# A fused adapter-linear and state-space kernel: an odd output sum moved ahead of a filter part, the next input loaded earlier, adapter sums held in the rows of their low part

## What is computed

```python
x = x + (einsum('bsd,od->bso', x, W) + bias + einsum('bsr,bor->bso', einsum('bsd,brd->bsr', x, A[ids]), B[ids]))
K = 2 * einsum('hn,hnl->hl', Ct, exp(dtA[:, :, None] * arange(L))).real      # 64 filters of 1024 taps
y = irfft(rfft(x, 2L) * rfft(K, 2L))[..., :L] + x * D[:, None]               # causal convolution
x = x + y * (arange(L) < length)
```

## Time and profile before

| | |
|---|---|
| median of 3 runs | 1104.22 us (1104.08 to 1106.7) |
| the profiled execution's own time | 1102.59 us |
| its span | 1100.9 us |
| mean granted TensorE clock | 0.998 |
| busy: PE, DVE, ACT, POOL | 97%, 77%, 65%, 2% of the span |
| DMA | 284.62 MB, mean 259 GB/s |

### The profile page before, as it was taken

How to read it: one execution, slowest core, us unless ns; L and a number is a source line. 1 busy time by engine, 2 the same in 40 slices (tenths; PEclk the granted TensorE clock), 3 DMA queues, 4 the chain that set the end, 5 groups by cost and what they waited for, 6 DMA issues and landing times.

```text
span 1100.9 us, 21550 instructions
## 1 busy us (share of the span) xinstructions
PE 1067.3 (97%) x8088; PEld 1031.4 (94%) x8088; DVE 848.3 (77%) x1263; ACT 715.7 (65%) x1260; POOL 27.4 (2%) x79
## 2 busy tenths in 40 slices
PE   9999999999999999999999999999999999999998
PEld 7999999999988999999999999999989999999997
DVE  7888877778687786768786777868478888888886
ACT  5655546655737546546647556556498888888885
POOL 0000000000000000000000000000000000000000
PEclk9999999999999999999999999999999999999999
DMA  8557768766867878867877868868799787879773
GB/s 306 192 180 290 259 197 280 230 258 211 288 176 284 245 254 274 231 230 230 269 236 247 253 234 285 232 231 250 264 306 356 285 338 282 344 270 357 280 274 132
DMA packets 162586, 284.62 MB, mean 259 GB/s; under 512 B 10739, under 2 KB 125620, under 8 KB 149044
## 3 DMA queue, kind: packets, MB, share of 16 engines
q1 hardware_dynamic: 162484, 283.26, 75.8%
HBM read 193.96 MB, written 89.26 MB: 257 GB/s over the span
## 4 chain that ended last, share of the span: by engine, by line
PE 68%; DVE 15%; ACT 7%; issue 4%; SPq 4%; DMA 2%; DVEq 0%; ACTq 0%
PE acc L1795 23%; PE acc L1955 23%; PE acc L1801 11%; DVE x_lo L1089 5%; PE acc L1723 4%; PE acc L1990 3%; PE acc L1767 2%; DVE x_sb L1245 2%; ACT L844 1%; DMA x_raw<-x_t 1%; ACT L857 1%; ACT t_hi L686 1%; SPq L436 1%; SPq L444 1%; SPq L440 1%
## 5 line engine op out<-in xcount | busy, mean ns | idle before, releaser
L686 ACT ACTIVATE acc<-acc 128x512 f32<-128x512 f32 x93 | 54.1, 584 | 129.4 <-PE acc L1801 129.1
L1795 PE MATMUL acc<-t_hi,w_pair 128*128 128x256 f32 x960 | 122.9, 280 | 7.0 <-issue 7.0
L1955 PE MATMUL acc<-u_hi,f_hi 128*128 128x512 f32 (+1 forms) x320 | 128.9, 403 | 0.0
L1795 PEld LDWEIGHTS acc<-t_hi,w_pair 128*128 128x128 f32 x960 | 116.8, 188 | 8.2 <-issue 8.2
L1795 PE MATMUL acc<-t_hi,v_lo 128*128 128x256 f32 x512 | 123.0, 279 | 0.0
L1795 PE MATMUL acc<-t_hi,v_hi 128*128 128x256 f32 x512 | 122.9, 279 | 0.0
L1955 PE MATMUL acc<-u_lo,f_hi 128*128 128x512 f32 (+1 forms) x320 | 118.3, 370 | 0.0
L1955 PE MATMUL acc<-u_hi,f_lo 128*128 128x512 f32 (+1 forms) x320 | 118.2, 369 | 0.0
L1089 DVE TENSOR_TENSOR x_lo<-x_raw,x_hi 128x512 fp32r<-128x512 f32 x128 | 79.9, 686 | 49.0 <-ACT x_hi L686 49.0
L1089 DVE TENSOR_TENSOR t_lo<-t_raw,t_hi 128x1024 fp32r<-128x1024 f32 x64 | 78.3, 1224 | 50.1 <-ACT t_hi L686 49.4
L1795 PE MATMUL acc<-x_hi,v_hi 128*128 128x256 f32 x384 | 93.6, 283 | 14.5 <-DVE x_sb L1245 14.3
(11 more groups left out here) (205 smaller groups left out, 2656.8 us busy)
## 6 DMA issues: line engine op xcount, KB each, us to landing
w_pair<-weight_scratch SPq DMA_DIRECT2D x71, 1024.0 KB, 6.2
x_scratch<-x_sb SPq DMA_DIRECT2D x32, 1024.0 KB, 6.3
out<-out_sb SPq DMA_DIRECT2D x63, 512.0 KB, 4.7
x_raw<-x_t SPq DMA_DIRECT2D x15, 2048.0 KB, 9.9
u_raw<-x_scratch SPq DMA_DIRECT2D x14, 2048.0 KB, 11.9
wq_raw<-state_scratch SPq DMA_DIRECT2D x16, 1024.0 KB, 7.8
a_raw<-lora_a SPq DMA_DIRECT2D x128, 64.0 KB, 1.9
b_raw<-lora_b SPq DMA_DIRECT2D x128, 64.0 KB, 2.3
```

The lines of the kernel that those rows point to most:

```text
L686: return act.activation(dst, src, ACT.Copy)
L1795: pe.matmul(by_row(bank_part(bank, i)), w[:, k, i, :], hi[:, k, :, :], start=opens and i == 0 and k == 0 and s == 0, stop=False, skip_grou ...
L1955: mm = pe.matmul(bank, w, m, start=first and i == 0, stop=last and i == 2, skip_group_check=onto_closed)
```

## The change

SP: the next x is loaded right after the S4 load of a group (x of group 1 ahead of the even blocks), the S1 load goes ahead of the A rows, and filter_stores(g, 2) and (g, 3) wait until after the B rows of the next group. ACT: four of the eight x_hi copies go ahead of the T4 split, seed_e(1) behind it; filter_step(g, 2) and (g, 3) behind seed_b(0) of the next group; in group 1 seed_c goes ahead; in the second stage take_state(3, 0) goes ahead of the residual of head 4. DVE: out_12(1) ahead of filter_step(g, 2). `h_own` leaves the x1 buffer and lies in the first rows of `hl`, so `take_h` no longer waits for the odd half's store, and the two subtractions of `split_h` wait for both copies and run one after the other.

```diff
-    h_own = place("h_own", [R2, N], F32, at=x1_at + X1_BYTES)
+    hl_at = cursor[0]
     hl = place("hl", [P, N], F32R)
+    h_own = place("h_own", [R2, N], F32, at=hl_at)
...
             load_filter_inputs()
+            load_x(1)
             load_blocks()
-            load_x(1)
...
                     load_b(i, row)
+                filter_stores(g - 1, 2)
+                filter_stores(g - 1, 3)
                 store_x1(g - 1, 1)
                 load_ws(g, S4)
                 if g < LAST:
+                    load_x(g + 1)
                     rows = [adapter_of(g + 1, i) for i in range(G)]
+                load_ws(g, S1)
+                if g < LAST:
                     sp.wait_ge(c_alo, 2 * (g + 1))
                     for i, row in enumerate(rows):
                         load_a(i, row)
-                load_ws(g, S1)
                 if g == 1:
                     store_sum(S4, 0)
                 filter_stores(g, 0)
-                if g < LAST:
-                    load_x(g + 1)
-                else:
+                if g == LAST:
...
                     store_x1(g, 0)
-                    filter_stores(g, 2)
-                    filter_stores(g, 3)
...
             def take_h(g):
                 act.wait_ge(m_h, 2 * (g + 1))
                 if g > 0:
-                    act.wait_ge(st_x1[1], 16 * g)
+                    act.wait_ge(m_21[1], g)
...
                 if p == 0:
                     act.wait_ge(c_blo, 2 * (g + 1))
                     act.wait_ge(st_x1[0], 16 * g)
-                else:
-                    act.wait_ge(c_hlo, 2 * (g + 1))
+                elif g > 0:
+                    act.wait_ge(st_x1[1], 16 * g)
...
+            for t in range(HALF):
+                split_x(1, t)
             take_p5(1, 0)
-            for t in range(NT):
+            for t in range(HALF, NT):
                 split_x(1, t)
             for g in range(1, n_groups):
                 out_21(1, g - 1)
                 seed_b(0, g)
+                filter_step(g - 1, 2)
+                filter_step(g - 1, 3)
...
                 if g == 1:
+                    seed_c(0, g)
+                    seed_c(1, g)
                     split_even(S3)
                 split_t(g, "T3")
                 if g == 1:
                     split_even(S1)
-                seed_c(0, g)
-                seed_c(1, g)
+                else:
+                    seed_c(0, g)
+                    seed_c(1, g)
...
                 seed_e(0, g)
+                if g < LAST:
+                    for t in range(HALF):
+                        split_x(g + 1, t)
+                split_t(g, "T4")
                 seed_e(1, g)
-                split_t(g, "T4")
                 filter_step(g, 1)
                 if g < LAST:
                     take_p5(0, g)
-                    for t in range(NT):
+                    for t in range(HALF, NT):
                         split_x(g + 1, t)
...
                 take_p5(1, g)
-                filter_step(g, 2)
-                filter_step(g, 3)
...
             split_filter(4)
+            take_state(3, 0)
             residual_early(4)
             residual_late(4)
-            for h in range(3, heads):
+            take_state(3, 1)
+            split_u_early(5)
+            split_u_late(5)
+            split_states(3, 0, 2)
+            split_filter(5)
+            take_state(3, 2)
+            split_states(3, 2, 3)
+            residual_early(5)
+            residual_late(5)
+            for h in range(4, heads):
...
             def split_h(g):
-                dve.wait_ge(c_hhi, 2 * g + 1)
-                for rows in (slice(0, R2), slice(R2, P)):
-                    minus_hi(hl[rows, :], h_own[:, :], hh[0:R2, :]).then_inc(c_hlo, 1)
+                dve.wait_ge(c_hhi, 2 * g + 2)
+                minus_hi(hl[R2:P, :], h_own[:, :], hh[0:R2, :]).then_inc(c_hlo, 1)
+                dve.wait_ge(c_hlo, 2 * g + 1)
+                minus_hi(hl[0:R2, :], h_own[:, :], hh[0:R2, :]).then_inc(c_hlo, 1)
...
             split_t(0, "T4")
+            for t in range(HALF):
+                split_x(1, t)
             out_12(1, 0)
-            for t in range(NT):
+            for t in range(HALF, NT):
                 split_x(1, t)
...
-                if g == 1:
-                    out_12(1, g)
-                    filter_step(g, 2)
-                else:
-                    filter_step(g, 2)
-                    out_12(1, g)
-                    filter_step(g, 3)
+                out_12(1, g)
+                filter_step(g, 2)
+                filter_step(g, 3)
```

## The result

| | before | changed |
|---|---|---|
| median of the runs (20 of each, same chip), us | 1103.55 | 1093.90 |
| lowest to highest, us | 1101.02 to 1106.70 | 1088.75 to 1103.87 |
| the profiled execution, us | 1102.6 | 1096.84 |
| its span, us | 1100.9 | 1095.1 |

The ratio is 0.9919, with a 95% interval of 0.9901 to 0.9938. The change gains about 9 us where the prediction had 25; 1093.9 lies above its range of 1075 to 1088. The changed kernel's 20 runs also scatter over 15 us, the 20 of the kernel before over 6.

The account below looks back on a forecast made before the run. PE is busy 97% of the span, so only its gaps can be won: 16.1 + 2.1 + 1.9 + 3.75 + 1.2 = 25.0 us off a 1104.2 us median gives 1079 us; 8 in 10 for 1075 to 1088.

Parts of the forecast that it names:

- Part 3: x loaded earlier: A22 lands in time for p4(0) in group 10, 2.1 us won; S1 and A rows behind x cost nothing.
- The other waits at p5(0) stay: PE's remaining waits at p5(0), ended by the chain from A-row split to taps, stay: 3.1 us not won.
- group 6: Stalls at end_11 and p5(0), behind a DVE and ACT chain that shortens: 1.9 us won beyond the out_12(1) term.
- Part 1: out_12(1) ahead of the third filter part on DVE: eleven PE waits at p1(1) go whole, 16.1 us.
- Part 4: Four x_hi copies ahead of the T4 split on ACT: they fit in idle time, cost nothing; uncovered, 29 us.
- Part 2: Adapter sums, take_h and hl before end_11: slack 1.2 us, nothing gained or lost; at worst 6 us over eleven groups.
- Start: Group 1, x issued ahead of the block loads: first stalls and low clock go, part returns at end_11; 3.75 us won.
- End: rotate(3, 0) on PE no longer waits for take_state(3, 0), now first on ACT: 1.2 us won.
- the wait moves on: Rival: DVE idles for take_p5(1), so out_22(1), T2 or taps are late; costs 6 to 8 us, 1087; chance 0.17.
- The slower rival: ACT waits for x ahead of the T4 split, delaying p4(0) in 14 groups: 29 us, 1108; chance 0.05.

Follow-up runs that it names:

- e1: Changed kernel with the A rows issued ahead of the next x, then x, then S1: 1096.6 us, ratio 0.9933.
- e2: Changed kernel with the load of x back at its old place, behind filter_stores(g, 0): 1078.9 us, ratio 0.9787.
- e9: Changed kernel with the A rows ahead of x and S1, and their splits late on ACT and DVE: 1096.0 us, ratio 0.9942.
- e4: Kernel before with one edit on DVE, out_12(1) ahead of filter_step(g, 2): 1094.3 us, ratio 0.9926.
- e8: Changed kernel with the A-row splits late on ACT and DVE and out_12(1) put back behind filter_step(g, 2): 1073.5 us, ratio 0.9725.
- e12: Changed kernel with x loaded at its old place and out_12(1) put back behind filter_step(g, 2): 1079.3 us, ratio 0.9790.
- e14: Changed kernel with out_12(1) put back behind filter_step(g, 2), run again beside the changed kernel on one chip: 1088.3 us, ratio 0.9876.
- e15: Kernel before with one edit on ACT, four x_hi copies ahead of the T4 split and seed_e(1) behind it: 1086.6 us, ratio 0.9857.
- e7: Changed kernel with the A-row splits late and x loaded at its old place, behind the filter stores: 1084.9 us, ratio 0.9813.
- e3: Changed kernel with the A-row splits moved behind filter_step(g, 0) on ACT and behind the T4 split on DVE: 1073.1 us, ratio 0.9736.
- e5: Changed kernel with only DVE's low parts of the A rows moved behind the T4 split: 1098.2 us, ratio 0.9941.
- e11: Changed kernel with out_12(1) put back behind filter_step(g, 2), nothing else: 1081.8 us, ratio 0.9828.
- e13: Changed kernel unaltered, run again: 1089.3 us, ratio 0.9864.
- e10: Changed kernel with 24 unread matmuls on PE ahead of its wait for the taps, in groups with taps: 1094.0 us, ratio 0.9929.
- e16: Changed kernel with both A-row splits late on ACT and DVE, run again unaltered: 1072.9 us, ratio 0.9728.
- e6: Kernel before with only the A-row splits moved late on ACT and DVE, nothing of the change: 1108.0 us, ratio 1.0031.

## Why the prediction was wrong

By its own steps, on its own basis: 1077.6 us for a profiled execution, against 1096.84, is 19.2 us.

- **Part 3, "the A rows now stand behind 2 MB of x ... I cost it at nothing": the step that failed.** It said that S1 and the A rows would be behind x, took the rule of order in a ring (the Trainium skill, DMA: Bandwidth & Descriptors, section Queues, rings and completion order) as speaking against the change, and then worked out the slack of S1 only. The rows' user is not PE but ACT, 18.9 us after down begins, with the filter's tables behind it and DVE's unit and the taps behind these. The first trace shows 18.4 - 4.2 = 14.2 us of new stall from it (4.2 being three times 0.45 and three times 0.95). The rule was right, and e1, e2 and e9 bear it out: the small transfer that stands behind x is late (rows 6.0 us to landing behind x and S1, 3.0 behind S1 alone, 1.9 ahead of both). The other half of Part 3 was right: A22's stall of 2.1 us is gone.
- **"The other waits at p5(0) stay ... nothing in it moves".** The 3.1 us did stay, as the 0.45 and 0.95 in the table (five of them, less the pitch of 0.12 each). But the sentence named the split of the A rows as the start of that chain and did not join it to the sentence above.
- **The clock after the new stalls, 8.7 us, was in no term.** The prediction had priced one such stretch, at the start, and no rival gave a long stall that surcharge. 14.2 + 8.7 = 22.9; group 6 took some 1.7 us less than the prediction had left there (0.45, pitch included, in place of 2.1), so 21.2 were to be missed and 19.2 were. The 2 us between are small gains, not all taken apart: where one of the eleven stalls went, a group fell by 0.1 us more than the stall (group 12 by 1.28 us for 1.17).
- **Part 1, 16.1 us: the size right, the edit that earns it wrongly named.** The eleven waits went whole, and the edit does remove them (e4). But alone it gives 8 us, and put back it costs nothing measurable (e8, e12, e14). **Part 4, costed at nothing,** removes the eleven waits by itself and gives 16.1 us (e15). Either is enough for these waits; that the sum came out for this part is luck. The prediction had the row in hand: 49.0 us of DVE waiting for x_hi, "some 3 us a group". It is now 0.5 us in all. It booked this as a cushion for Part 1 and for group 6, and never asked whether DVE would then reach out_12(1) in time where it stood. Part 4's danger, T4 late at p4(0), did not show with x early; it did in e7, with x late.
- **Part 2, adapter sums: right.** In group 4 of the changed kernel hl is done at 217.92 and end_11 begins at 221.76; no take_h waits for a DMA. The slack was larger than the 1.2 us worked out, and the rival's 0.5 us a group did not come.

```profile
216.52 1.40 DVE L1108 TENSOR_TENSOR hl<-h_own,hh 64x512 fp32r<-64x512 f32 x2 [1.35 <-ACT hh L687]
```
```profile
221.76 0.28 PE L1785 MATMUL acc<-hh,b_st 128*128 128x256 f32 x1
```

- **Start 3.75 us: right.** From the first matmul of down in group 0 to that in group 2 it was 91.5 us and is 87.5: 4.0 us. No low clock is left there, and end_11 of group 1 waits 1.4 us, 1.6 with the 0.16 added, as forecast.
- **End 1.2 us: half.** The wait for take_state(3, 0) went from 1.3 to 0.7 us.
- **Of the rivals,** "the wait moves on" had the right form and the wrong place. It looked for the next late thing on the engines (T2, out_22, taps behind a longer DVE), and what came late was a transfer, in front of ACT. Its 6 to 8 us were also too small without the clock. The slower rival, x late on ACT, did not occur in the change: ACT waits 1.2 us in all for x.

## What to carry to other kernels

When a large load moves up in a queue, list everything that is then behind it, small transfers first, and follow each to the engine that uses it and to what stands behind that use; the slack to compare with is that of the chain's end. If the consumer can go behind the work that matters, do that rather than move the load (e3: no transfer moved, 20 us won). When an engine stands 3 us a group waiting for another, cure that first: it may be the whole of a stall further down that looks like an order problem. And look at the spread of the runs: the versions in which PE hung on the landing of a transfer (changed, e1, e5, e9, e11, e13, e14) scattered over 4 to 15 us, and e3, e10 and e16 over less than 1. One trace of such a version, or a comparison of two of them that did not run side by side, can mislead by 12 us.

## What the runs showed of the hardware

- A 64 KB row landed in 1.9 us (median) in the kernel before and in e1, where x was issued behind the rows; in 3.0 us behind a 1 MB load on the same queue (e2); in 6.0 us behind 2 MB and 1 MB (changed).
- Granted clock and stalls, from start to start, the last few us of a run left out. All 13 stalls of 3.19 to 5.43 us, in six of the traces, had 3.4 or 6.8 us at half clock with them or behind them. Between 2.17 and 3.12 us both occur: 2.17 us in e5 and 2.41 in e14 were followed by a low stretch; 2.49 in e14, 3.12 in e13 and the stall of the earlier trace rows, 3.01, were not. Below 2.17 us none was, but for group 1 of e6, where the clock fell at two stalls of 1.31 and 1.85 us within 3 us. No length in these traces divides them cleanly.
- Filling the same idle time with 24 matmuls that nobody reads kept the clock at 1.00 until the last few us (e10).
